# Voting makes of the routing stage issued in nine runs of four that cross lane ends

## The reference

```python
priors = jnp.einsum('nfdhwij,ofijud->nhwofiju', patches, weight)
logits = jnp.zeros_like(priors)
for r in range(NUM_ITERATIONS):                 # 3
    probs = jax.nn.softmax(logits, axis=-3)
    out = jnp.sum(probs * priors, axis=-2, keepdims=True)
    if r != NUM_ITERATIONS - 1:
        out = squash(out)
        logits = logits + jnp.sum(priors * out, axis=-1, keepdims=True)
```

## Time and profile before

| | before |
|---|---|
| median of 3 runs | 13054.74 us (13053.78 to 13056.06) |
| the profiled execution, its own time | 13062.33 us |
| its span in the trace | 13060.4 us |
| TensorE's mean granted clock in it | 0.971 |
| routing stage in the span | from about 90 to 4060 us |

### The profile page before, as it was taken

One profiled execution on the slowest core, in us unless ns is written; L12 is line 12 of the kernel. 1 busy time (PEld: TensorE's weight loads), 2 busy tenths in 40 slices (PEclk: granted clock), 3 DMA queues, 4 the chain that ended last, 5 costly groups with the idle time before them and its releaser, 6 DMA issues. The chain is left out here.

```text
span 13060.4 us, 254754 instructions
## 1 busy us (share of the span) xinstructions
PE 12457.9 (95%) x73276; PEld 4722.7 (36%) x73276; DVE 9306.3 (71%) x17387; ACT 7464.9 (57%) x14966; POOL 3121.0 (24%) x3012
## 2 busy tenths in 40 slices
PE   6999999999996499999999999999999999999899
PEld 2333333333332133333333333333333333333233
DVE  6777777777777577777777777777777777777311
ACT  3555555555554166666666666666666666666411
POOL 4666566656654000000000000000000000000143
PEclk9999999999998599999999999999999999999999
DMA  3101111010112523323223232332322322223255
GB/s 77 22 15 22 19 18 22 15 22 15 22 21 57 130 63 73 69 65 75 66 69 71 66 71 68 71 71 63 75 67 66 74 66 70 70 66 73 66 124 109
DMA packets 853454, 772.37 MB, mean 59 GB/s; under 512 B 587092, under 2 KB 621492, under 8 KB 840884
## 3 DMA queue, kind: packets, MB, share of 16 engines
q1 hardware_dynamic: 850612, 747.43, 25.2%
q10 hardware_dynamic: 1536, 8.39, 0.3%
HBM read 510.63 MB, written 244.96 MB: 58 GB/s over the span
## 5 line engine op out<-in xcount | busy, mean ns | idle before, releaser
L1509 DVE TENSOR_REDUCE a_big<-a_mp 128x1 f32<-128x512 f32 x8192 | 5220.5, 685 | 1824.1 <-PE a_mp L1343 1805.9
L1429 ACT ACTIVATE a_ex<-a_sc 128x512 f32<-128x512 f32 x8192 | 4426.3, 600 | 1934.8 <-PE a_sc L1331 1929.6
L1343 PE MATMUL a_mp<-a_ks,a_qs 108*128 108x512 bf16 x8192 | 3131.1, 383 | 39.4 <-DMA a_ks<-qk_parts 24.9
L1331 PE MATMUL a_sc<-a_qs,a_ks 111*128 111x512 bf16 x8192 | 3124.5, 383 | 6.8 <-ACT a_ex L1429 4.3
L859 DVE TENSOR_TENSOR r_prod<-r_pg,r_win 128x512 f32<-128x512 f32 x3072 | 2020.2, 684 | 833.7 <-PE r_pg L597 479.1
L525 POOL TENSOR_TENSOR r_prod<-r_temp,r_win 128x512 f32<-128x512 f32 x1536 | 1801.9, 1188 | 1608.3 <-ACT r_temp L816 1593.6
L1357 PE MATMUL a_po<-a_ex,a_va 128*32 128x512 f32 x16384 | 2181.9, 605 | 1.4 <-ACT a_oc L1435 0.7
L1245 POOL TENSOR_TENSOR a_pieces<-a_left,a_pieces 128x512 bf16<-128x512 f32 x256 | 295.8, 1156 | 7323.4 <-ACT a_pieces L1415 7323.4
L1331 PEld LDWEIGHTS a_sc<-a_qs,a_ks 111*128 111x128 bf16 x8192 | 794.9, 97 | 2477.5 <-ACT a_ex L1429 1767.9
L1343 PEld LDWEIGHTS a_mp<-a_ks,a_qs 108*128 108x128 bf16 x8192 | 803.2, 98 | 913.2 <-DVE a_big L1509 237.6
L597 PE MATMUL r_pg<-r_stack,r_wv 32*128 32x512 f32 x4608 | 1006.1, 642 | 22.9 <-DVE r_prod L859 22.1
(11 more groups left out here) (184 smaller groups left out, 11659.3 us busy)
## 6 DMA issues: line engine op xcount, KB each, us to landing
a_qs<-qk_parts SPq DMA_DIRECT2D x768, 144.0 KB
a_ks<-qk_parts SPq DMA_DIRECT2D x768, 144.0 KB
qk_parts<-a_pieces SPq DMA_DIRECT2D x128, 768.0 KB, 5.2
f_t<-mixed SPq DMA_DIRECT2D x48, 1536.0 KB, 16.5
a_tw<-second SPq DMA_DIRECT2D x512, 128.0 KB, 3.0
mixed<-a_t SPq DMA_DIRECT2D x256, 256.0 KB, 2.1
r_win<-first SPq DMA_DIRECT2D x128, 280.5 KB, 5.1
a_zw<-layered SPq DMA_DIRECT2D x192, 144.0 KB, 12.1
```

The lines of the kernel that those rows point to most:

```text
L1331: pe.matmul(sc[k % BANKS][:, :], ks[0:KROWS + NPART, p.h, head, 128 * kb:128 * kb + 128], qs[0:KROWS + NPART, p.h, head, CHUNK * qb:CHUNK ...
L1343: pe.matmul(mp[k % BANKS][:, :], qs[0:KROWS, p.h, head, 128 * q:128 * q + 128], ks[0:KROWS, p.h, head, CHUNK * half:CHUNK * half + CHUNK], ...
L1429: nc.scalar.activation(ex[:, k % RING, :], sc[k % BANKS][:, :], ACT.Exp, scale=scale).then_inc(exped.sem, 1)
L1509: nc.vector.tensor_reduce(big[:, x % 2, k // 2:k // 2 + 1], mp[k % BANKS][:, :], AX_X, ALU.max).then_inc(maxed.sem, 1)
```

## The change

The 36 makes of a quartet (four lanes of nine) are no longer issued as four, four and one in each lane's slot. They become nine runs of four, counted through without regard to where a lane ends. The slot of lane 0 issues three runs and those of lanes 1 to 3 two each, so that the third run in lane 0's slot holds lane 0's position 8 and lane 1's positions 0, 1 and 2. The row group is counted through in the same way. The slots that sum keep their runs of four, four and one. On ACT the copy of the first squash transpose moves behind the copies of positions 0 and 1, in all slots. The rules of the ring are not changed, and no instruction's work is.

```diff
             if voting:
 
-                q = slice(32 * (pos % 4), 32 * (pos % 4) + 32)
+                group = (TAPS * lane + pos) % 4
+                q = slice(32 * group, 32 * group + 32)
                 last = pe.matmul(bank[:, :], wv[q, 128 * tap:128 * tap + 128], stack[q, lane, :],
-                                 start=True, stop=True, tile_position=(32 * (pos % 4), 0))
+                                 start=True, stop=True, tile_position=(32 * group, 0))
...
+        def run(p, s, heavy, k):
+
+            if not heavy:
+                return
+            lane = s % LANES
+            if s % 8 >= LANES:
+                makes = ((0, 4), (4, 8), (8, 9))[k]
+            elif lane == 0:
+                makes = ((0, 4), (4, 8), (8, 12))[k]
+            else:
+                makes = ((4 - lane, 8 - lane), (8 - lane, 12 - lane if lane < 3 else 9), (0, 0))[k]
+            for pos in range(*makes):
+                make(p.n, s + pos // TAPS, pos % TAPS)
...
-            for pos in range(4):
-                if heavy:
-                    make(p.n, s, pos)
+            run(p, s, heavy, 0)
...
-            for pos in range(4, 8):
-                if heavy:
-                    make(p.n, s, pos)
+            run(p, s, heavy, 1)
...
-            for pos in range(8, 9):
-                if heavy:
-                    make(p.n, s, pos)
+            run(p, s, heavy, 2)
...
             back = [x for x in lights(s, "C", ("squash",)) if x[0] in which]
-            for d, kind, r, lane, part in back[:1]:
-                finish_squash(p.to(d), r, lane)
             own = sorted(POOLED, key=ORDER.index) if heavy else []
...
             for g in own[:2]:
                 evacuate_make(g)
+            for d, kind, r, lane, part in back[:1]:
+                finish_squash(p.to(d), r, lane)
```

## The result

| | before | after |
|---|---|---|
| median of 4 runs each, us | 13055.4 | 13554.75 (13546.9 to 13564.72) |
| ratio, with its 95% interval | | 1.0382 (1.0364 to 1.04) |
| span of the profiled execution, us | 13060.4 | 13551.7 |

The change costs 499 us. The time lies inside the predicted range, 55 us above the predicted 13,500. First the page of the changed kernel: busy time, share of the span and instructions of each engine.

What follows compares the result with a forecast made beforehand. PE's queue was taken to set the pace. Bank waits of 13.11 us a pass over 32 passes (420 us) plus clock falls (27 us) make 447 us, added to the profiled 13,062: some 13,500 us, range 13,370 to 13,690.

Steps and rivals of the forecast that it cites:

- Bank waits in PE's queue: In slots 0 to 3 and 8 to 11, earlier makes wait for banks still being read: 13.11 us a pass, 420 us.
- The walk: Slots 8 to 11 timed make by make, 6.35 us a pass lost; slots 0 to 3 likewise, 6.76 us.
- The walk's one rule: When a run's last make is released at t, PE goes on at t + 1.19 us.
- What ended PE's idle time: In front of L598: DVE in slots 0, 3, 8 and 11, ACT's L823 in slots 1, 2, 9 and 10.
- No gain from fewer makes: Dropping slot 11's single make wins nothing: slot 12's batch 1 is held 5.29 us after slot 11's second run.
- ACT's new order: Frees second runs of slots 8 to 10 from 0.57 us each; in the other slots it costs nothing.
- The clock: Thin first runs of slots 2, 3, 10 and 11 lower PE's clock: one fall every second pass, 27 us.
- a clock well below 1.00 in the voting slots: One of two signs that would show the prediction wrong; the other was voting slots shorter than 7.3 us.
- Half hidden: Rival: position 4's copy is in time, second runs of slots 1, 2, 9 and 10 lose nothing: 13,305 us; chance 0.08.
- Falling clock: Rival: every thin run of slots 2, 3, 10 and 11 lowers the clock, 218 us: 13,690 us; chance 0.18.
- Faster: Rival: bank waits do not bind, PE saves 8.0 us a pass, 256 us: 12,800 us; chance 0.05.
- No change: Rival: waits and savings cancel, 13,055 us; chance 0.03.

Runs made afterwards that it cites:

- experiment 3: Changed kernel, with ACT copying position 4 ahead of the logit copies in the slots of lanes 1 to 3: 13488.52 us.
- experiment 8: Changed kernel with POOL's wait, experiment 3, experiment 4, DVE's positions 7 and 8 early in lanes 1 to 3, batch 0 before slots 0 and 8's third run: 13051.95 us.
- experiment 10: Kernel of experiment 9, with DVE taking positions 7 and 8 early in lane 0 too: 12948.78 us.
- experiment 11: Kernel of experiment 10, with DVE's early positions 7 and 8 in lanes 0 to 2 only: 12946.72 us.
- experiment 6: Kernel before, with POOL's wait and ACT's new order, no makes crossing lanes: 12947.76 us.
- experiment 1: Kernel before, with only ACT's new order and no makes crossing lanes: 13053.72 us, ratio 0.9998.
- experiment 9: Kernel of experiment 8, with batch 0 of slots 0 and 8 put back behind their third run: 13015.43 us.
- experiment 12: Kernel of experiment 10, with DVE's early positions 7 and 8 in lanes 0 and 1 only: 13052.81 us.
- experiment 5: Kernel before, with POOL's wait and nothing else: 12952.43 us, ratio 0.9921.
- POOL's wait: POOL's products held, in a slot where DVE ends a squash, until that is done; added to the changed kernel: 13417.77 us.
- experiment 4: Changed kernel, with ACT copying the next lane's positions 0 and 1 (slots 2 and 10: position 0) in the slot that makes them: 13546.96 us.

## Why the prediction was right, and what it mis-sized

**Bank waits in PE's queue: right.** The walk's slots came out one by one. Slot 9 lasted 8.40 us (walk 8.58), slot 10 9.54 (9.78), and slot 12's first batch stood 5.24 behind slot 11's second run (5.29). Experiments 3, 8 and 10 brought readers forward, and the time of the slots that the walk had put on these readers fell: with all of them in time the crossing's 470 us are gone. These are the causes shown. The walk's one rule was a little long: its 1.19 us was read where the third make of a run was the late one. Where the last is, PE goes on sooner: in slot 8's third run DVE's product ended at 2171.63 and the next instruction started at 2172.73, 1.10 later.

**What ended PE's idle time: right but for one place.** In the pass shown the rows name DVE at the runs of slots 8 and 11 and ACT's L823 in slot 9 and in slot 10's second run. In slot 10's first run the row names DVE's product, which I had put beside the later copy. The run's last make comes where I had put it, behind L784 (it starts at 2183.42) and a copy:

```profile
2184.63 0.29 PEld L598 LDWEIGHTS r_pg<-r_stack,r_wv 32*128 32x128 f32 x2 [0.30 <-ACT r_temp L823]
```

**No gain from fewer makes: right, and more so than said.** Even with every named wait mended, taking out the six single makes (6.3 us a pass) comes with a gain of only 0.29 us: the voting slots sum to 55.90 us in experiment 11 and to 56.19 in experiment 6. Slots 3 and 11 stay at 7.04, held by a product, as the walk had it for slot 11. Elsewhere runs of four still stretch, so the readers, not PE's own work, set what is left.

**ACT's new order: wrong.** The step "ACT's new order in the other slots I cost at nothing" and the statement that DVE's busy time stays the same both fail: DVE has 257 us more. The walk also booked 0.57 us in each of slots 8 to 10 for this order. Alone, the order gave nothing (experiment 1); slot 7's interval, 0.51 longer in the changed kernel and in experiment 1, and slot 14's are where it comes out. I had looked at what ACT's copies release on PE, and not at what they start on POOL.

**The clock: right in kind, too small.** I entered one fall in every second pass, 27 us. In 30 passes the clock fell 41 times in the four runs that I had named (19 in slot 2, none in slot 3, 5 in slot 10, 17 in slot 11), where I had entered 15. What a voting slot's mean stands above its shortest interval is the clock's, as the 30 passes show: 2.99 us a pass after (slots 0, 1, 2 and 11 have nearly all of it) and 0.84 before, so 2.15 times 32, some 69 us. The prediction had called a clock well below 1.00 in the voting slots a sign of being wrong. That sign came, in more than half of the passes of slots 2 and 11; it falls on this term, not on the bank waits. The rule of the Trainium skill that the prediction weighed ("TensorE: Matmul & The Clock Gate", section "A second HAM failure mode: psum-queue depth-cycling") speaks of such swings; the traces agree that they come, in some passes and not in others. Why one of two like runs lets the clock fall and the other does not stays open.

**The sum, and the luck in it.** The shortest intervals of the voting slots grew by 12.58 us a pass, 403 us where the walk had 420. The clock in them adds 69, slot 14 19, slot 7 16, slot 15 5, and slot 6, whose clock falls less often, takes away 12: 500 us. So the bank waits, 17 us too long in the walk, were offset by slot 7's 16 us, which it had put at nothing. That part of the nearness is luck; the 52 us by which the measured loss exceeds 447 are the clock in the main.

**The other rivals.** *Half hidden* fell: position 4's copy was late, and taking it forward won 66 us. *Falling clock* came in part: 41 falls of the 120 that it needed, and 69 us in the voting slots where it had 218. *Faster* fell on the readers; experiments 8 to 12 moved the readers that the walk had named and reached no more than a tie. *No change* fell with the 499 us.

**What stays open.** Slot 14 takes one of several values between about 10.3 and 14.2 us, from kernel to kernel and from pass to pass, and moved the totals by up to 86 us. These values go with the clock. Two passes of the kernel of experiment 5 (columns as in rows 1):

```profile
2060.36:2070.79 10.43, 8.46 (x60) 3.37 (x56) 10.11 (x22) 5.87 (x11) 3.47 (x3) 1.00 0.01 2
1936.36:1948.53 12.17, 11.20 (x61) 4.35 (x57) 10.58 (x24) 5.88 (x11) 3.47 (x3) 0.72 0.00 0
```

In all kernels with POOL's wait slot 14 takes 10.4 us in passes at 1.00 and 11.9 to 12.7 in passes at 0.71 to 0.74. Without the wait the clock in it is 0.76 or lower in every pass, and PE waits there for a late DVE product besides. What decides whether the clock falls in a pass is open, and no run was made for it alone.

## What to carry to other kernels

In a ring of few buffers, ask of every make that is issued earlier whose read it now waits for, and walk the slots with the row times: that gave each slot to a quarter of a microsecond. Look at what an earlier copy starts on the engine behind it, too, as a helper engine that starts sooner can block the one that matters. A wait that keeps GpSimd out of a short VectorE chain won 0.8% here, about half of it by a clock that fell less often, and every version that ties as the fastest (12,947 to 12,952 us) has it; the crossing, with or without mends, is not needed for it.

## What the runs showed of the hardware

**DVE is held by POOL's whole instruction.** A DVE multiplication of 128 x 128 with both operands in SBUF took 0.29 us alone and 1.22 when POOL's product (two SBUF operands, 1.17 us each) had started ahead of it. Over the stage its mean went from 292 ns (POOL kept away) over 524 (before) to 1224 in the changed kernel:

```profile
L932 DVE TENSOR_TENSOR r_sq<-r_cap,r_fac 128x128 f32<-128x128 f32 x245 | 299.8, 1224 | 8.4
```

DVE's products out of PSUM kept 0.69 us beside the same POOL instructions, and POOL's kept their 1.17. The Trainium skill states this in "SBUF — State Buffer", section "Who interferes with whom": a VectorE instruction with two SBUF inputs contends with a GpSimd instruction that reads SBUF, and the ports that they share are an exclusive lock, so that the order of issue decides which of the two is blocked. The trace agrees, with the ends of the two DVE rows that lie within 0.14 us of the ends of POOL's two products; all 254 long multiplications of the changed kernel end within 0.16 us of the end of one. A DVE instruction with one SBUF operand was held as well: in experiment 4 the addition behind the square (TENSOR_SCALAR, 128 x 16) rose from a mean of 174 to 310 ns, and the 63 long ones of 256 all ended 0.03 us behind a product of POOL that had started ahead of them.

**One late make costs its own wait.** With 1.19 us from a late make's release to the next instruction, read from one row of before, the walk came within 0.25 us of the shortest interval of every voting slot; a run that waits in its last make is delayed by that wait and not by the time of a second run.
